# Solving the removal system in 32x64 tiles, with R turned on VectorE: one attention layer with a mixture of experts on one core

## What is computed

```python
def step(s, inp):
    q_, w_, k_, v_, a_, b_ = inp
    sa = jnp.einsum('bhij,bhj->bhi', s, a_)
    s = s * w_[:, :, None, :] + sa[..., None] * b_[:, :, None, :] + v_[..., None] * k_[:, :, None, :]
    return (s, jnp.einsum('bhij,bhj->bhi', s, q_))
_, y = jax.lax.scan(step, s0, (qt, wt, kt, vt, at, bt))
```

## Time and profile before

| | us |
|---|---|
| median of 3 runs | 1091.34 |
| the three runs | 1085.73, 1091.34, 1097.99 |
| the profiled execution | 1092.08 |
| its span (first to last instruction) | 1090.1 |

### The profile page before, as it was taken

The page is one execution under the profiler, slowest core; times in us unless marked ns, Lnnn a source line. Parts: engine busy times, 40 slices in busy tenths (PEclk is TensorE's granted clock), DMA queues, the critical chain, the costliest instruction groups (busy, mean ns, idle before and its releaser), DMA issues.

```text
span 1090.1 us, 42536 instructions
## 1 busy us (share of the span) xinstructions
PE 1016.1 (93%) x16804; PEld 833.7 (76%) x16805; DVE 778.8 (71%) x1777; ACT 542.1 (50%) x1113; POOL 612.6 (56%) x1135
## 2 busy tenths in 40 slices
PE   8898999999999999999999999679899999999995
PEld 5675777787776776777777777566798888989894
DVE  4775887888787977888878877247566666666663
ACT  4474676686585775766766757222122222222220
POOL 1087786787776875877868868640223232323321
PEclk9998999999899998999999999689999999999998
DMA  4113224134133242242251341838454454545430
GB/s 104 41 20 79 71 35 107 42 71 107 25 89 90 33 100 60 52 109 57 56 106 28 86 100 18 234 86 289 179 184 165 163 180 153 186 146 181 147 127 4
DMA packets 208625, 112.02 MB, mean 103 GB/s; under 512 B 172365, under 2 KB 191953, under 8 KB 208081
## 3 DMA queue, kind: packets, MB, share of 16 engines
q1 hardware_dynamic: 202080, 100.77, 34.3%
q0 software_dynamic: 3744, 8.40, 2.3%
q10 hardware_dynamic: 2640, 0.54, 0.2%
HBM read 85.42 MB, written 26.08 MB: 102 GB/s over the span
## 4 chain that ended last, share of the span: by engine, by line
PE 80%; DMA 5%; DVE 4%; issue 4%; POOL 3%; ACT 1%; SPq 1%; DVEq 0%; POOLq 0%; ACTq 0%
PE bank L561 20%; PE bank L950 12%; PE bank L963 9%; PE bank L699 6%; PE bank L646 6%; PE bank L654 5%; PE ry L963 4%; PE bank L607 4%; PE ry L676 3%; PE ry L728 2%; PE bank L716 2%; PE ry L682 2%; POOL arena L1906 2%; POOL arena L1903 2%; PE bank L579 1%
## 5 line engine op out<-in xcount | busy, mean ns | idle before, releaser
L1906 POOL TENSOR_TENSOR arena<-arena 128x30 f32<-128x30 f32 (+14 forms) x480 | 258.9, 539 | 37.6
L1903 POOL TENSOR_TENSOR arena<-arena 128x30 f32<-128x30 f32 (+14 forms) x480 | 252.8, 527 | 36.4
L561 PE MATMUL bank<-arena 128*128 128x256 f32 (+2 forms) x992 | 267.3, 406 | 4.9 <-DVE arena L1405 2.4
L561 PEld LDWEIGHTS bank<-arena 128*128 128x128 f32 x992 | 171.2, 194 | 49.5 <-issue 25.1
L950 PEld LDWEIGHTS bank<-arena 128*128 128x128 f32 x1248 | 145.3, 192 | 5.5 <-issue 2.7
L950 PE MATMUL bank<-arena 128*128 128x128 f32 x1248 | 145.8, 275 | 3.2 <-DVE arena L1812 2.5
L1489 DVE TENSOR_TENSOR arena<-bank,arena 128x512 f32<-128x512 f32 x128 | 79.6, 684 | 34.1 <-PE bank L646 34.1
L1293 ACT ACTIVATE arena<-arena 128x1 f32<-128x1 f32 x39 | 11.5, 295 | 176.5 <-DVE arena L1766 176.5
L963 PE MATMUL bank<-arena 128*128 x416 | 96.4, 385 | 0.1
L1937 POOL COPY arena<-arena 128x1 int32 (+1 forms) x39 | 7.1, 183 | 144.8 <-DVE arena L1830 144.8
L963 PEld LDWEIGHTS bank<-arena 128*128 128x128 f32 x416 | 76.9, 190 | 14.4 <-issue 4.9
(11 more groups left out here) (174 smaller groups left out, 1806.8 us busy)
## 6 DMA issues: line engine op xcount, KB each, us to landing
arena<-in_W SPq DMA_DIRECT2D x47, 1024.0 KB, 5.0
scr_n<-arena SPq DMA_DIRECT2D x64, 128.0 KB, 2.7
arena<-scr_n SPq DMA_DIRECT2D x16, 512.0 KB, 4.0
scr_u<-arena SPq DMA_DIRECT2D x16, 512.0 KB, 2.9
arena<-scr_u SPq DMA_DIRECT2D x62, 128.0 KB, 2.9
arena<-in_xTp SPq DMA_DIRECT2D x32, 132.0 KB, 4.0
arena<-in_x SPq DMA_DIRECT2D x64, 64.0 KB, 2.2
scr_x<-arena SPq DMA_DIRECT2D x64, 64.0 KB, 2.7
```

The source lines that it names most:

```text
L561: mm = pe.matmul(ring.tile(m, name)[0:rows, to], lhsT, rhs, start=(i == 0), stop=(i == len(terms) - 1))
L1903: inv_ok.inc(f"m{s}", TT(t, U[:, 0:s, s:s + 1].broadcast_to(shape), U[:, s:s + 1, s + 1:TB].broadcast_to(shape), ALU.mult))
L1906: inv_ok.inc(f"a{s}", TT(U[:, 0:s, s + 1:TB], U[:, 0:s, s + 1:TB], t, ALU.add))
```

## The change

R is turned by VectorE: `keep_r` now transposes it in 32x32 squares from PSUM into `Rs`, which has half the words of `Rm`. `turn_r` and `keep_rt` are gone, and with them the jobs `rt0` and `rt1`. `Ux` is laid out by pair: 32 partitions (times) hold the 64 columns of a pair's two heads. `solve(m, w)` has 32 matmuls of 32 rows x 64 stationary columns x 32 moving columns for the pairs 2w and 2w+1; they go in turn over two row groups and both column halves, into the banks `xa@1` and `xb@3`. `solve(n-1, 0)` stands where `turn_r` stood, `solve(n-1, 1)` where it was; the `solve` between projection v and the turns is gone. Since each product has both heads' channels, the other head is masked in the copy: VectorE multiplies three quarters of X by `same_head` (`xae`, `xao`, `xbo`), ScalarE scales the fourth by `own_head` in two copies (`xb0`, `xb1`). `x_kept` waits for all five. `update(n-1, 1)` moves ahead of `scores(n+1, 0)`. The DRAM scratch of scores and inverse is ordered by pair, and one more small tensor (`head_mask`) is loaded at the start.

```diff
-        Rm_flat = take(NB // 2 * P)
-        RT = [take(4 * P).rearrange("p (k n) -> p k n", k=4) for _ in range(HALF)]
+        Rs = take(NB * TB).rearrange("p (e g i) -> p e g i", e=2, g=NB // 2)
...
-        nd = nc.dram_tensor("scr_n", (HALF, PAIRS, 4, 2, 2 * TB, TB), F32, kind="Internal").ap()
+        nd = nc.dram_tensor("scr_n", (PAIRS, 4, HALF, 2, 2 * TB, TB), F32, kind="Internal").ap()
...
-        chain_dve = Stage(sem("chain_dve"), [(-1, "rme rmo x1o x0o")])
+        chain_dve = Stage(sem("chain_dve"), [(-1, "re ro xae xao xbo")])
...
-        chain_act = Stage(sem("chain_act"), [(-1, "rt1 rt0 x1e x0e ye yo")])
+        half_solved = sem("half_solved")
+        chain_act = Stage(sem("chain_act"), [(-1, "xb0 xb1 ye yo")])
...
-                            (-2, "g@0"), (1, "ma@5 mk@2"), (-1, "rt0@3 rt1@4"), (-2, "wo@0"), (-1, "x1@1"),
-                            (1, "ss@0 r@4"), (0, "bk11@5"), (1, "v@2"), (-1, "x0@3"), (0, "bk10@5 v0@1 v1@4"),
+                            (-2, "g@0"), (1, "ma@5 mk@2"), (-1, "xa@1 xb@3"), (-2, "wo@0"),
+                            (1, "ss@0 r@4"), (0, "bk11@5"), (1, "v@2"), (0, "bk10@5 v0@1 v1@4"),
...
-                for e in range(2 if m < last else 1):
-                    for h in range(2):
-                        at_row = 64 * (1 - e) + TB * h
-                        sp.dma_start(Ux[m % 2][at_row:at_row + TB, :, :, :, h, :], u_rows[e, h]).then_inc(u_in, 16)
+                for p in range(PAIRS if m < last else 2):
+                    sp.dma_start(heads_of(m, p), u_rows[p]).then_inc(u_in, 16)
...
-            def solve(m, f):
-                ring.wait_empty(pe, m, f"x{f}")
-                chain_act.wait(pe, m, f"rt{f}")
-                pe.wait_ge(u_in, (m + 1) * 64)
-                for k in range(B // 2):
-                    for p in range(PAIRS):
-                        for e in range(2):
-                            x, at = x_rows_of(e), k * P + 32 * p
-                            mm = pe.matmul(ring.tile(m, f"x{f}")[x, at:at + 32], Ux[m % 2][x, f, p, k].rearrange("p h t -> p (h t)"),
-                                           RT[f][x, k, 32 * p:32 * p + 32], start=True, stop=True)
-                ring.fill(m, f"x{f}", mm)
+            def solve(m, w):
+                if w == 0:
+                    for bank in "ab":
+                        ring.wait_empty(pe, m, f"x{bank}")
+                    chain_dve.wait(pe, m, "re", "ro")
+                    pe.wait_ge(u_in, (m + 1) * 64)
+                else:
+                    pe.wait_ge(half_solved, m + 1)
+                mm = {}
+                for g in range(NB // 2):
+                    for turn in range(2):
+                        for i, bank in enumerate("ab"):
+                            e, r = (turn + i) % 2, pair_rows(2 * w + i)
+                            at = (w * NB // 2 + g) * 32
+                            mm[bank] = pe.matmul(ring.tile(m, f"x{bank}")[x_rows_of(e), at:at + 32],
+                                                 Ux[m % 2][r, g % 4, g // 4, e].rearrange("p h t -> p (h t)"), Rs[r, e, g, :],
+                                                 start=True, stop=True)
+                if w == 1:
+                    for bank in "ab":
+                        ring.fill(m, f"x{bank}", mm[bank])
+                else:
+                    mm["b"].then_inc(half_solved, 1)
...
-                if has(n - 1):
-                    turn_r(n - 1, 0)
-                    turn_r(n - 1, 1)
+                if has(n - 1) and n - 1 < last:
+                    solve(n - 1, 0)
...
+                if n - 1 == last:
+                    solve(n - 1, 0)
...
-                if has(n - 1):
-                    solve(n - 1, 0)
...
+                if has(n - 1) and n - 1 < last:
+                    update(n - 1, 1)
                 if has(n + 1):
                     scores(n + 1, 0)
...
-                if has(n - 1) and n - 1 < last:
-                    update(n - 1, 1)
...
-            def keep_rt(m, f):
...
+            def keep_x(m):
+                ring.wait_full(act, m, "xb")
+                x = x_rows_of(0)
+                for h in range(2):
+                    i = slice(HS * h, HS * h + HS)
+                    chain_act.inc(m, f"xb{h}", A(solution_home(m, 1, 0)[:, :, :, i], solution(m, "xb", 0)[:, :, :, i], ACT.Copy,
+                                                 scale=own_head[x, h:h + 1]))
...
-                    chain_dve.inc(m, f"rm{name}", TT(Rm[:, :, 1 - e], RY[e][:, :, 0, None, :].broadcast_to(shape),
-                                                     odd_even[:, None, :, None].broadcast_to(shape), ALU.mult))
+                    chain_dve.inc(m, f"r{name}", nc.vector.transpose(Rs[:, e], RY[e][:, :, 0]))
...
+            def keep_x(m, bank, e):
+                ring.wait_full(dve, m, f"x{bank}")
+                chain_dve.inc(m, f"x{bank}{'eo'[e]}", TT(solution_home(m, "ab".index(bank), e), solution(m, f"x{bank}", e),
+                                                         same_head[x_rows_of(e), None, None, :].broadcast_to([P // 2, 2, NB // 2, 32]),
+                                                         ALU.mult))
...
-                    keep_x_odd(n - 1, 1)
+                    keep_x(n - 1, "a", 0)
+                    keep_x(n - 1, "a", 1)
...
-                    keep_x_odd(n - 1, 0)
+                    keep_x(n - 1, "b", 1)
```

More of the change, by code:

```diff
@@ L361, in build @@
         freed.update({f"v{f}": [(turned, f"v{f}e"), (turned, f"v{f}o")] for f in range(HALF)})
[L362 removed]
+        freed["xa"] = [(chain_dve, "xae"), (chain_dve, "xao")]
+        freed["xb"] = [(chain_act, "xb0"), (chain_act, "xb1"), (chain_dve, "xbo")]
         filled = [sem(f"filled{i}") for i in range(len(banks))]
         ring = Ring(banks, [(0, "bk00@5"), (1, "h@2 k@3"), (0, "bk01@2"), (1, "z@1 a@4 kk@5"), (-3, "logit@2"),
[2 rows of a table removed]
[2 rows of a table added]
                             (1, "rk@3"), (-1, "su@0"), (1, "sc00@2 sc01@5 sc02@3 sc03@1 tg@4"), (2, "lo1@5"),
@@ L1230, in body @@
                 if n == last + 1:
-                    odd_inverse_to_heads(last)
-                if has(n - 1):
-                    keep_rt(n - 1, 1)
+                    second_inverse_to_heads(last)
                 if has(n + 1):
```

83 lines of the change are left out of this document (35 added, 48 removed).

## The result

| | before | after |
|---|---|---|
| median, us | 1093.66 | 1205.18 |
| ratio after / before, 95% interval | | 1.1028 [1.0968, 1.1089] |
| span of the profiled execution | 1090.1 | 1202.0 |

The change makes the kernel 10% slower; the forecast was 1111 us, the range ended at 1130. (Single executions far above the others, 2379 us of after's four and 5133 us of e17's four, are left out of the ratios, though not of the medians, which would be 1204 and 1111 us without them.) First the page of after: busy times, then TensorE's clock in 40 slices. The line of before is in the earlier trace rows.

What follows compares the result with a forecast made beforehand. The prediction took the kernel as TensorE-bound (93% busy), VectorE's chain 0.7 us behind; `read_out` 1.47 us later in 13 full blocks gave 19.1, added to the profiled 1092.1: 1111 us, range 1085 to 1130.

Steps and rivals of the forecast that it cites:

- `update`'s move: `update(n-1, 1)`, 0.69 us, only swaps places with `scores(n+1, 0)`, `gate_1` and `low_1`: costs nothing.
- TensorE's price of the solve: 64 records of a half solve take 1.0 us with four array tiles at once, for 1.99 before.
- Transposes: VectorE's two transposes of R, 0.87 us for both, at worst 1.21 each, hide behind the wait for `gates`: no cost.
- The waits ahead of the moved solve: `solve(n-1, 0)` waits for bank 1 (the scan) and the inverse, 1.75 us on the mean, 1.05 to 2.4.
- w: Wait ahead of the moved solve, the later of bank 1 and the inverse: 1.75 us mean a block.
- VectorE's chain: From `project_out`'s end to X's last copy, 10.05 us mean with one more copy; `read_out` then starts 1.47 us later a block.
- T: Start of `turn_r` in a block, where the moved solve then stands; `read_out` forecast at T + 14.60 for T + 13.13.
- Clock and gaps: Idle time a block may hide gaps or lower the clock: bounded by -1.0 and +1.2 us, taken as 0 together.
- the clock falls in most blocks: Rival: the clock falls at the new waits, 1.2 us more a block, 1127 us; chance 0.14.
- Blocks 14 and 15: Block 14: 0, solve's saving against the interposed `project_out`; block 15: -0.8 us, left out of the sum.
- The inverse's distance: The inverse's DMAs keep count, sizes and descriptors, so its landing keeps its distance from T, T + 1.54 on the mean.
- Block 0: The first block has no `project_out` and waited for the inverse already: 0.

Runs made afterwards that it cites:

- e17: After with both moves undone and SyncE's queue split, plus VectorE's `decay_kk` and `removal` behind the last copy of X: 1116 us, ratio 1.024.
- e9: After with the loops of `solve` swapped, so that two array tiles are in turn instead of four: 1229 us (one).
- e4: Before with one addition: TensorE waits for the scan and the inverse ahead of `turn_r`: 1124 us, ratio 1.029.
- e7: Before with only `update(n-1, 1)` moved ahead of `scores(n+1, 0)`: 1144 us, ratio 1.049.
- e1: After with only `update(n-1, 1)` put back between `low_1` and the second scores: 1153 us, ratio 1.054.
- e13: After with both moves undone and SyncE's order split (inverse written, tokens' loads, inverse read, x1 stored): 1101 us, ratio 1.005.
- e10: After with SyncE's issues reordered, the inverse ahead of the loads of tokens and stores of x1: 1181 us, ratio 1.085.
- e8: After with `update(n-1, 1)` back, plus 4 matmuls whose result nobody reads ahead of the moved solve: 1136 us, ratio 1.044.
- e3: After with matmuls whose result nobody reads in three waits (first solve, projection v, a turn of values): 1202 us, ratio 1.093.
- e12: After with both moves undone, plus 3 matmuls whose result nobody reads ahead of the solve: 1119 us, ratio 1.023.
- e16: After with both moves undone and SyncE's queue split, plus matmuls nobody reads in two waits ahead of `read_out`: 1100 us, ratio 1.006.

## Why the prediction was wrong, step by step

The kernels give the loss in steps: 1205 us for after, 1153 without `update`'s move, 1121 without both moves, 1101 with SyncE's order split as well, 1094 for before.

**TensorE's price of the solve: right.** 64 records in 1.13 us (1.06 packed) for the 1.0 forecast, 16.6 ns each; e9 shows 1.85 with two tiles. The Trainium skill's rule in "TensorE: Matmul & The Clock Gate", Part 3, The mechanism, that a weight load overlaps matmuls only of another row group, would have given 2.0; the 1.06 goes against it. The Trainium skill, "TensorEngine Tiling (Array Packing)", Key Properties, lets different tiles load weights and multiply in parallel; the 1.06 agrees.

**Transposes: right.** 0.77 us for both, hidden behind the wait for the gates.

**The waits ahead of the moved solve: right in kind, 0.6 too small.** 1.03 us for the scan in three blocks, up to 3.65 for the inverse in the others, 2.38 on the mean over the 13 blocks for w = 1.75. The same wait in before (e4) is 1.94, so 0.2 of the 0.6 is the sum's own error; the other 0.4 came with the change, and why is open.

**VectorE's chain: right.** With w = 1.03 the prediction's own sum gives T + 1.03 + 1.0 + 1.73 + 10.05 + 0.07 = T + 13.88; the undisturbed block at T = 499.23 has 513.18, T + 13.95. The wait of 2 to 3 us that I placed at `read_out` came as two of 1.1, at projection v (bank 2, freed by L1411) and at a turn of values (bank 4, freed by `bonus_terms`, L1431), because the banks are freed by the same chain.

**Clock and gaps, taken as 0 a block: the step that failed.** The waits forecast were 1.75 + 2.7 = 4.45 us a block; those with a cause rose by 4.07. Against them stand 2.86 us less work. Without the clock and the gaps a block would be 1.2 us longer; 1.47 was forecast. The rest is idle time without a cause, 3.44 us a block for 1.64 (1.27 of the 1.80 are gaps, 0.53 the wait of 0.58), and 9.96 us more at half clock, which costs half of that, 4.98. TensorE's busy time says nearly the same: it rose by 1.94 while 2.86 of work went, 4.80. Sum: 4.07 + 1.80 + 4.98 - 2.86 = 7.99; measured 7.77. I had the earlier trace rows, which shows a fall behind an idle time of 1.25 us, and bounded the loss by 1.2 a block. The bound was from one fall; e4 shows that each wait of 1.96 us or more brought one. The rival "the clock falls in most blocks" named the mechanism, had 0.14, and its price, 1.2, was a fifth of what came (6.8).

The Trainium skill, "TensorE: Matmul & The Clock Gate", HAM oscillation, puts the loss at the throttled time times one half; the sum above bears that out.

**`update`'s move, costed at nothing: the second step that failed.** It "only swaps places" with the scores and the gates, I wrote, and looked at who is served later, not at what the 0.7 us lay in front of. It covered a wait of 0.58 us, and ahead of the scores it lengthens the row in which the gaps arise. Alone 49 us (e7), undone 52 (e1).

**Blocks 14 and 15, taken as 0: 3 us, the sum of two errors.** Block 14 came out 2.5 us shorter, by luck: a gap of 4.26 us in before's `read_out` was 0.83 in after, while the solves, apart and at half clock, and the copies behind them took 1.6 more. Block 15, which I took as 0.8 better, is 5.5 longer. Its solve waits 1.07 us for the inverse and has a gap of 1.46, and two masked copies on VectorE are now serial between the last solve and `read_out`, which waits 2.18 us for them (0.17 before).

```profile
843.27 1.72 PE L745 MATMUL ry<-arena 128*32 128x32 f32 x113 [2.18 <-DVE arena L1508]
```

**The inverse's distance: only partly right.** "Their count, sizes and descriptors stay, so the distance stays": the landing did (2.9 us in the median, as the earlier trace rows), but that SyncE's order was worth 20 us with the late solve (e13), and another order 24 in after (e10), I did not ask.

**Block 0, taken as 0: 4.6 us.** No run took it apart.

## What to carry to other kernels

Before work is taken off or moved ahead of a wait, ask of each moved piece what it stands in front of, and price a wait of 2 us on TensorE at up to twice its length unless something else keeps the engine busy (e4: 1.4 to 2.2 times). A step that "only swaps places" costs the wait that it covered, and what the clock makes of that wait. When a DMA's landing becomes the last wait, look at the order of the issues in its queue before looking at its size: here that order was worth 20 us.

## What the runs showed of the hardware that I had not expected

- A wait of 1.03 to 1.17 us ahead of `turn_r` left the clock at 2.4 GHz in five blocks of e4, and so did 1.63 and 1.76 us; in six waits of 1.96 to 3.41 us it fell to 1.2 GHz, during the wait or at most 0.94 us behind it. Elsewhere short idle times were followed by 1.2 GHz too (5 of 13 in before).
- Dead matmuls can pay: some 2 us a block of them took half clock from 5.97 to 1.71 us and 19 us from the 12 blocks (e8 against e1). Elsewhere they gave 4 us or nothing: in three waits of after, where the gaps stayed (e3), and where the waits are short (e12, e16).
- Rows of small matmuls have gaps for which no releaser shows, up to 2.5 us in the full blocks of e7 and 4.26 in block 14 of before, mostly one or two a block. They end at the same place of every 256 records (matmuls and weight loads), mostly where the 256 had run in under 3.0 us: 505 of 566 idle times without a releaser in the 18 traces. Nothing that I tried removed them without a wait in their place.
